# Delta rule: VectorE inverts the first chunk's diagonal blocks, GpSimd begins with the second chunk

## The chip, the cores and the metric

The kernel runs on one core of one Trainium2 chip. The metric is the device time of one execution in microseconds (us); the median of three runs of the kernel before is 3021.94 us (3019.69 to 3023.62). Engines are TensorE (PE), VectorE (DVE), ScalarE (ACT), GpSimd (POOL) and SyncE (SP), which here issues all DMAs. Each engine works through its own queue in order, and they wait for one another on semaphores.

## The reference, cut to what matters

Two layers on a stream of 2 x 1024 tokens of 512 features, each sublayer behind a layernorm and added to the stream: attention by a gated delta rule, a feed-forward with 4-bit weights, latent attention, a sparse feed-forward. The change is in the first. Its core, per batch and head (6 heads of 64):

```
def step(S, inputs):
    q_t, k_t, v_t, g_t, b_t = inputs
    S = S * exp(g_t)
    kv = einsum('bhk,bhkv->bhv', k_t, S)
    u = b_t * (v_t - kv)
    S = S + einsum('bhk,bhv->bhkv', k_t, u)
    o_t = einsum('bhk,bhkv->bhv', q_t * scale, S)
```

over all 1024 steps.

## The kernel before, in words

`four_sublayers` runs the sublayers one after another. In the first, `project_front` computes the projections and writes the convolved q, k and v to a tensor in HBM; `delta_rule` then does the recurrence in 8 chunks of 128 steps (`CHUNKS`), for 12 pairs of batch and head (`BH`) together. Within a chunk the recurrence is a triangular system of 128 unknowns per pair. Its matrix is built from key products (`key_blocks` on VectorE, line 1491, into `a_t`), and query products give `att` (`query_blocks`, line 1500). The four diagonal blocks of 32 x 32 (`BASE`) of each of the 12 matrices are inverted directly; the rest is done on TensorE.

The diagonal blocks travel so. SyncE's `take_blocks(c)` waits until VectorE has written all 12 matrices of the chunk (`a_done`), copies the blocks to HBM (line 912) and back as `base_l`, one block to a partition (line 914): 4 x 12 = 48 partitions, 0 to 47 for even chunks and 64 to 111 for odd ones (`base_rows`). `start_base` has put identity matrices into `base_t`. GpSimd then runs 31 steps of elimination. Step j multiplies column j of `base_l` by row j of `base_t` into `base_tmp` (line 979) and subtracts that from the rows below (line 984), both over (31 - j) x (j + 1) elements of each partition, each instruction waiting for the one before it. At a chunk's end it raises `base_done`. ScalarE transposes the result (`turn_blocks`, line 1312, `tt_done`), and SyncE's `give_blocks(c)` writes both to HBM (line 924) and scatters them into the block-diagonal `diag` and `diag_t` (line 930). TensorE's `off_blocks(c)` (line 1087) waits for `diag`, and `apply_blocks(c)` (line 1118) for `diag_t`.

The order on each engine is written out by hand. The chunks 0 and 1 are prepared in a prologue; turn c of the main loop then solves chunk c and prepares chunk c + 2.

- SyncE: `take_blocks(0)`, load of chunk 2, `take_blocks(1)`, `give_blocks(0)`; then in turn c a load, `take_blocks(c + 2)`, `give_blocks(c + 1)`.
- GpSimd: three memsets, then the inversion of chunks 0 to 7.
- VectorE: for the chunks 0 and 1 the norms, `values_and_keys`, `key_blocks`, `query_blocks`; then `w_lo` (line 1617); then turn 0, which begins with `decay_queries(2)` (line 1434), with `refine_solution(0, ...)` (line 1510) behind it and `norms(2)` (lines 1411 to 1468).
- ScalarE: after its part of the prologue it copies the decayed queries of chunk 1 (line 1304), casts `w_hi` (line 1371), waits for `w_lo_done`, and only then does `turn_blocks(0)`; turn 0 follows with the squares of chunk 2's queries (line 1275) and `copy_off_blocks` (line 1323).
- TensorE: in the prologue, after the query products of chunk 1, `turn_decayed_queries(1)` (line 1073), which waits for eight of VectorE's query blocks; turn 0 begins with `turn_queries(2)`, which waits for all twelve, and `off_blocks(0)`.

Of the kernel before, what the change touches and what calls it, by code (L numbers as in the profile page):

```python
# [23 lines left out]
ALU = mybir.AluOpType  # L24
# [91 lines left out]
def inverse_deviation(pool, norm, rows, group):  # L116

    pool.wait_ge(norm.moments, 7 * group + 7)
    pool.tensor_tensor(norm.rstd[:, rows], norm.var[:, rows], norm.power[:, rows], ALU.pow).then_inc(norm.rstd_done, 1)
# [308 lines left out]
CHUNKS = SEQ // CHUNK  # L428
# [3 lines left out]
BASE = 32  # L432
# [337 lines left out]
def delta_rule(nc, stream, ident, mask, hidden, qkv, beta, decay, eye, w_out, token_norm, fp4, codes, scales):  # L770
# [10 lines left out]
    with Scope(nc, "dr", give_back=True) as s:  # L781
# [3 lines left out]
        NB = QUARTERS * BH  # L785
# [18 lines left out]
        a_t = fp4.weight[:].rearrange("p u (h t) -> p u h t", t=P)  # L804
        base_l, base_t = s.sb("base_l", [P, BASE, BASE]), s.sb("base_t", [P, BASE, BASE])
        base_tt, base_tmp = s.sb("base_tt", [P, BASE, BASE]), s.sb("base_tmp", [P, BASE * BASE // 4])
        diag, diag_t = s.sb("diag", [P, BH, P]), s.sb("diag_t", [P, BH, P])
        m_t = s.sb("m_t", [P, BH, P])
        z = s.sb("z", [P, 2, BH, HEAD_DIM0])
# [15 lines left out]
        l_out, l_in = s.sem("l_out"), s.sem("l_in")  # L825
        t_init = [s.sem(f"t_init{u}") for u in range(2)]
        t_out, tt_out, diag_in, diag_t_in = (s.sem(x) for x in ("t_out", "tt_out", "diag_in", "diag_t_in"))
        w_hi_done, w_lo_done, const_done, zero_done = (s.sem(x) for x in ("w_hi_done", "w_lo_done", "const_done", "zero_done"))
# [5 lines left out]
        d_ps, d_done, kk_ps, qk_ps, a_done, att_done = (s.sem(x) for x in ("d_ps", "d_done", "kk_ps", "qk_ps", "a_done", "att_done"))  # L834
        evens_done = s.sem("evens_done")
        qg_ps, qg_copied = s.sem("qg_ps"), s.sem("qg_copied")
        base_step, base_done, tt_done = s.sem("base_step"), s.sem("base_done"), s.sem("tt_done")
        y_ps, y_done, m_ps, m_done = (s.sem(x) for x in ("y_ps", "y_done", "m_ps", "m_done"))
        z_ps, z_done, w_ps, w_done, x_ps, x_done = (s.sem(x) for x in ("z_ps", "z_done", "w_ps", "w_done", "x_ps", "x_done"))
# [39 lines left out]
        def base_rows(c):  # L879

            return slice(64 * (c % 2), 64 * (c % 2) + NB)
# [9 lines left out]
        STEPS = 2 * (BASE - 1)  # L891
# [72 lines left out]
        @block.gpsimd  # L964
        def _(pool):
            pool.memset(diag[:], 0.0).then_inc(zero_done, 1)
            pool.memset(diag_t[:], 0.0).then_inc(zero_done, 1)
            pool.memset(m_t[:], 0.0).then_inc(zero_done, 1)
            for c in range(CHUNKS):
                rows = base_rows(c)  # L970
                pool.wait_ge(l_in, 16 * (c + 1))
                pool.wait_ge(t_init[c % 2], 16 * (c // 2 + 1))
                for j in range(BASE - 1):
                    left, done = BASE - 1 - j, j + 1
                    shape = [NB, left, done]
                    update = base_tmp[rows, 0:left * done].rearrange("p (r c) -> p r c", r=left)
                    if c or j:
                        pool.wait_ge(base_step, STEPS * c + 2 * j)
                    pool.tensor_tensor(update, base_l[rows, j, j + 1:].unsqueeze(2).broadcast_to(shape),  # L979
                                       base_t[rows, j, 0:done].unsqueeze(1).broadcast_to(shape),  # L980
                                       ALU.mult).then_inc(base_step, 1)
                    pool.wait_ge(base_step, STEPS * c + 2 * j + 1)
                    target = base_t[rows, j + 1:, 0:done]
                    pool.tensor_tensor(target, target, update, ALU.subtract).then_inc(base_step, 1)
                pool.wait_ge(base_step, STEPS * (c + 1))
                pool.sem_inc(base_done, 1)
            pool.memset(token_norm.power[:], -0.5).then_inc(token_norm.power_done, 1)
            pool.wait_ge(token_norm.power_done, 1)
            inverse_deviation(pool, token_norm, EARLY, 0)
# [414 lines left out]
        def _(dve):  # L1404
# [22 lines left out]
            def decay_queries(c):  # L1427
                if c:
                    dve.wait_ge(qg_ps, 2 * c)
                else:  # L1430
                    dve.wait_ge(e_all_done, 1)
                for b in range(BATCH):
                    dve.wait_ge(q_squared, 2 * c + b + 1)
                    dve.tensor_tensor(heads(q_gt[:, b, :]), bank_of_heads(2 + b), along(e_of(0, b, c)),
                                      ALU.mult).then_inc(qg_done, 1)

            def sum_queries(c):
                dve.wait_ge(q_squared, 2 * c + 2)
                dve.tensor_reduce(sums[:, 0, :], square[:, 0].rearrange("p b (h d) -> p (b h) d", d=HEAD_DIM0),
                                  AX.X, ALU.add).then_inc(summed, 1)  # L1440

            def decay_keys(c, b):
                dve.wait_ge(k_squared, 2 * c + b + 1)
                dve.tensor_tensor(rhs[:, c % 3, 1, own(b), :], bank_of_heads((4, 2)[b]), along(e_of(0, b, c)),
                                  ALU.mult).then_inc(bk_done, 1)

            def sum_keys(c):
                dve.wait_ge(k_squared, 2 * c + 2)
                dve.tensor_reduce(sums[:, 1, :], square[:, 1].rearrange("p b (h d) -> p (b h) d", d=HEAD_DIM0),
                                  AX.X, ALU.add).then_inc(summed, 1)  # L1450
                dve.wait_ge(summed, 3 * c + 2)
                dve.tensor_scalar(sums[:], sums[:], 1e-6, None, ALU.add).then_inc(summed, 1)
                dve.wait_ge(summed, 3 * c + 3)
                dve.reciprocal(weight[:], sums[:, 1, :]).then_inc(small, 1)
                dve.wait_ge(small, 6 * c + 1)
                dve.tensor_tensor(by_batch(weight), by_batch(weight), of_chunk(beta[:], c), ALU.mult).then_inc(small, 1)
                dve.wait_ge(small, 6 * c + 2)
                dve.tensor_tensor(by_batch(k_weight), by_batch(weight),
                                  of_chunk(e_all[:, 1, :].rearrange("p (i h) -> p i h", h=HEADS0), c),
                                  ALU.mult).then_inc(small, 1)  # L1460
# [21 lines left out]
            def key_blocks(c):  # L1482
                dve.wait_ge(d_done, FOURS * c + 3)
                if c >= 2:
                    dve.wait_ge(m_ps, FOURS * (c - 1))
                    dve.wait_ge(l_out, 16 * QUARTERS * (c - 1))
                for g, group in enumerate(GROUPS):
                    dve.wait_ge(kk_ps, FOURS * c + g + 1)
                    for i in group:
                        place = PLACE[i][1] * P  # L1490
                        dve.scalar_tensor_tensor(out=a_t[:, c % 2, i, :], in0=banks[KK_BANKS[g]][:, place:place + P],
                                                 scalar=weight[:, i:i + 1], in1=att[:, c % 3, i, :],
                                                 op0=ALU.mult, op1=ALU.mult).then_inc(a_done, 1)

            def query_blocks(c):
                for g, group in enumerate(GROUPS):
                    dve.wait_ge(qk_ps, FOURS * c + g + 1)
                    for i in group:
                        place = PLACE[i][1] * P
                        dve.scalar_tensor_tensor(out=att[:, c % 3, i, :], in0=banks[QK_BANKS[g]][:, place:place + P],  # L1500
                                                 scalar=weight[:, i:i + 1], in1=att[:, c % 3, i, :],
                                                 op0=ALU.mult, op1=ALU.mult).then_inc(att_done, 1)
# [86 lines left out]
            def first_codes(nibble, ops):  # L1589
# [12 lines left out]
                if 2 in ops:  # L1602
                    dve.wait_ge(fp4.step, at + 2)
                    fp4.scaled(dve, nibble).then_inc(fp4.step, 1)

            for c in range(2):
                decay_queries(c)
                sum_queries(c)
                for b in range(BATCH):
                    decay_keys(c, b)  # L1610
                sum_keys(c)
                norms(c)
                values_and_keys(c)
                key_blocks(c)
                query_blocks(c)
            dve.wait_ge(w_hi_done, 1)
            dve.tensor_tensor(w_lo[:], w32, w_hi[:].bitcast(F32), ALU.subtract).then_inc(w_lo_done, 1)
# [1284 lines left out]
```

## Time and profile before

| | |
|---|---|
| median of three runs | 3021.94 us |
| the profiled execution | 3021.52 us |
| its span (first to last instruction) | 3019.7 us |
| busy in it: PE, DVE, ACT, POOL | 94%, 56%, 36%, 26% |
| delta rule, main loop | about 240 to 560 us |
| chunk 0's inversion on GpSimd | ends at about 239.6 us |

Times in the rows are microseconds from the start of the span. A row of the view in order of time gives start, duration from the first of its instructions to the last, engine, line, operation, output and inputs, how often, and in square brackets how long the engine sat idle before it and what ended that. SPq is SyncE's queue issuing DMAs. Releasers are inferred from semaphore events.

### The profile page before, as it was taken

To read this page: it belongs to the slowest core of one execution; us is meant where nothing else is said; L and a number is where in the kernel's file an instruction comes from. 1 tells how busy PE (TensorE), PEld (TensorE's weight loads), DVE (VectorE), ACT (ScalarE), POOL (GpSimd) and SP (SyncE) were. 2 spreads that over 40 slices of the span, in tenths; PEclk is the share of its full clock that TensorE was granted. 3 is DMA by queue.
4 is the path that set the end of the run, shared out by engine and by line. 5 is a ranking of instruction groups with operands and counts; after the bars stand their busy time and mean duration, and the time that the engine had idled before them with its cause. 6 is when DMAs were issued, how large, how long until landed. Compare 5 with 4: busy or idle time off the path is not lost. (4 is left out here: it accounts for less than half of the span.)

```text
span 3019.7 us, 37185 instructions
## 1 busy us (share of the span) xinstructions
PE 2829.2 (94%) x13750; PEld 2332.9 (77%) x13750; DVE 1702.2 (56%) x2585; ACT 1073.9 (36%) x1615; POOL 791.4 (26%) x832
## 2 busy tenths in 40 slices
PE   7966988799999999999999689999999899999998
PEld 7846777678888888888888558888888677888887
DVE  6864677564445444454543666666666256545554
ACT  3343343131121211111211357777777522212221
POOL 0038686100000000000000157777778510000000
PEclk9967999899999999999999889999999999999999
DMA  2243232110000100000100121111110100101001
GB/s 85 104 115 70 52 73 49 46 42 21 22 21 21 42 21 21 21 21 21 35 7 1 40 64 43 43 43 36 43 36 22 43 14 28 42 1 42 14 14 42
DMA packets 96418, 114.92 MB, mean 38 GB/s; under 512 B 47072, under 2 KB 73696, under 8 KB 94624
## 3 DMA queue, kind: packets, MB, share of 16 engines
q1 hardware_dynamic: 96288, 113.20, 12.7%
q8 instruction: 80, 1.31, 0.2%
q14 instruction: 50, 0.41, 0.0%
HBM read 86.16 MB, written 26.74 MB: 37 GB/s over the span
## 5 line engine op out<-in xcount | busy, mean ns | idle before, releaser
L2017 POOL TENSOR_TENSOR att_p_lo<-att_probs,att_p_hi 128x768 fp32r<-128x768 f32 x256 | 467.3, 1837 | 147.3 <-ACT att_p_hi L2074 146.1
L2170 DVE TENSOR_REDUCE att_top<-att_q_scores 128x1 f32<-128x1024 f32 x250 | 305.5, 1222 | 220.0 <-PE att_q_scores L2277 187.9
L271 DVE TENSOR_TENSOR fp_hidden<-fp_gelu,fp_up 128x512 f32<-128x512 f32 x128 | 88.0, 687 | 440.2 <-PE fp_up L75 377.2
L2085 ACT ACTIVATE att_probs<-att_k_scores 128x1024 f32<-128x1024 f32 x256 | 262.9, 1027 | 160.9 <-PE att_k_scores L2295 159.5
L1751 POOL MEMSET lat_power<- 128x16 f32 x1 | 0.1, 111 | 1051.8 <-POOLq L52 1051.8
L256 DVE TENSOR_TENSOR k_stream<-k_stream,fp_down 128x512 f32<-128x512 f32 x256 | 175.4, 686 | 89.6 <-PE fp_down L75 86.1
L335 ACT ACTIVATE fp_gelu<-fp_gate 128x512 f32<-128x512 f32 x128 | 76.4, 597 | 420.3 <-PE fp_gate L75 419.4
L2074 ACT CAST att_p_hi<-att_probs 128x768 fp32r<-128x768 f32 x256 | 211.7, 827 | 0.0
L73 PE MATMUL fp_gate<-fp_feat_hi,fp_w_hi 128*128 128x512 f32 x512 | 200.6, 392 | 4.0 <-DVE fp_feat_lo L241 4.0
L2277 PE MATMUL att_q_scores<-att_k_stack,att_q_stack 128*128 128x512 f32 x500 | 187.1, 456 | 14.5 <-DMA att_q_stack<-att_k_stack 10.6
L75 PE MATMUL fp_gate<-fp_feat_hi,fp_w_lo 128*128 128x512 f32 x512 | 200.2, 391 | 0.0
L74 PE MATMUL fp_gate<-fp_feat_lo,fp_w_hi 128*128 128x512 f32 x512 | 200.1, 391 | 0.0
L73 PE MATMUL fp_up<-fp_feat_hi,fp_w_hi 128*128 128x512 f32 x512 | 199.4, 389 | 0.0
L74 PE MATMUL fp_up<-fp_feat_lo,fp_w_hi 128*128 128x512 f32 x512 | 199.4, 389 | 0.0
L73 PE MATMUL fp_down<-fp_w_hi,fp_h_hi 128*128 128x512 f32 x512 | 199.3, 389 | 0.0
L75 PE MATMUL fp_up<-fp_feat_hi,fp_w_lo 128*128 128x512 f32 x512 | 199.2, 389 | 0.0
L75 PE MATMUL fp_down<-fp_w_hi,fp_h_lo 128*128 128x512 f32 x512 | 199.2, 389 | 0.0
L74 PE MATMUL fp_down<-fp_w_lo,fp_h_hi 128*128 128x512 f32 x512 | 199.2, 389 | 0.0
L2616 DVE TENSOR_TENSOR la_values<-sp_silu,sp_up 128x512 f32<-128x512 f32 x64 | 43.9, 687 | 226.2 <-PE sp_up L75 225.3
L2295 PE MATMUL att_k_scores<-att_q_stack,att_k_stack 128*128 128x512 f32 x512 | 165.0, 403 | 1.7 <-DVE att_top L2170 1.3
L2314 PE MATMUL att_out_rest<-att_probs,att_whole_values 128*128 128x256 f32 x512 | 152.0, 378 | 0.0
L979 POOL TENSOR_TENSOR dr_base_tmp<-dr_base_l,dr_base_t 48x31 f32<-48x31 f32 (+15 forms) x248 | 124.9, 504 | 89.2 <-DMA dr_base_l<-blocks_l 70.1
(350 smaller groups left out, 6537.3 us busy)
## 6 DMA issues: line engine op xcount, KB each, us to landing
f_early<-codes SPq DMA_DIRECT2D x16, 768.0 KB
f_early<-scales SPq DMA_DIRECT2D x16, 768.0 KB
la_values<-w_sparse SPq DMA_DIRECT2D x10, 1024.0 KB, 5.2
f_early<-qkv SPq DMA_DIRECT2D x16, 576.0 KB, 6.2
att_q_stack<-rotated SPq DMA_DIRECT2D x128, 64.0 KB, 2.6
att_k_stack<-rotated SPq DMA_DIRECT2D x128, 64.0 KB, 2.6
qkv<-f_early SPq DMA_DIRECT2D x12, 512.0 KB, 2.9
k_stream<-hidden SPq DMA_DIRECT2D x4, 1024.0 KB, 10.3
```

The costliest lines, as they stand in the source:

```text
L73: pe.matmul(out, w_hi, x_hi, start=start, stop=False)
L74: pe.matmul(out, w_hi, x_lo, start=False, stop=False)
L75: return pe.matmul(out, w_lo, x_hi, start=False, stop=stop)
L256: dve.tensor_tensor(tile, tile, down_ps[j][:], ALU.add).then_inc(added, 1)
L979: pool.tensor_tensor(update, base_l[rows, j, j + 1:].unsqueeze(2).broadcast_to(shape), base_t[rows, j, 0:done].unsqueeze(1).broadcast_to(s ...
L2017: pool.tensor_tensor(p_lo[:, buffer, :], probs[:, slot, 0:SPLIT], p_hi[:, buffer, :].bitcast(F32), ALU.subtract).then_inc(lo_done, 1)
L2074: act.copy(p_hi[:, buffer, :], probs[:, slot, 0:SPLIT]).then_inc(hi_done, 1)
L2085: act.activation(probs[:, t, :], k_scores[:], ACT.Exp).then_inc(exp_done, 1)
L2170: dve.tensor_reduce(top[buffer][:, STACK + t:STACK + t + 1], scores[:], AX.XY, ALU.max, negate=True).then_inc(max_done, 1)
L2277: last = pe.matmul(scores[:, half, :], q_stack[j][:, t * P:(t + 1) * P], k_stack[j][:, half * TB:(half + 1) * TB], start=True, stop=True)
L2295: last = pe.matmul(k_scores[:, half, :], k_stack[j][:, t * P:(t + 1) * P], q_stack[j][:, half * TB:(half + 1) * TB], start=True, stop=True)
L2314: pe.matmul(out_rest[:, 1, 0:REST], whole_values[:, buffer, t, :], probs[:, t, SPLIT:], start=t == 0, stop=t == T - 1).then_inc(out_done, 1)
```

## The change

VectorE gets a function `first_base` with the same 31 steps for chunk 0, on the same tensors and partitions, and calls it in its prologue between `key_blocks(1)` and `query_blocks(1)`. GpSimd's loop over chunks starts at 1; before it stands a wait for its own memsets, and before chunk 1's increment of `base_done` a wait for chunk 0's. The semaphore `first_step` orders the new instructions.

```diff
             pool.memset(m_t[:], 0.0).then_inc(zero_done, 1)
-            for c in range(CHUNKS):
+            pool.wait_ge(zero_done, 3)
+            for c in range(1, CHUNKS):
...
-                    if c or j:
-                        pool.wait_ge(base_step, STEPS * c + 2 * j)
+                    if c > 1 or j:
+                        pool.wait_ge(base_step, STEPS * (c - 1) + 2 * j)
...
-                pool.wait_ge(base_step, STEPS * (c + 1))
+                pool.wait_ge(base_step, STEPS * c)
+                if c == 1:
+                    pool.wait_ge(base_done, 1)
                 pool.sem_inc(base_done, 1)
...
+            def first_base():
+                rows = base_rows(0)
+                dve.wait_ge(l_in, 16)
+                dve.wait_ge(t_init[0], 16)
+                for j in range(BASE - 1):
+                    left, done = BASE - 1 - j, j + 1
+                    shape = [NB, left, done]
+                    update = first_tmp[rows, 0:left * done].rearrange("p (r c) -> p r c", r=left)
+                    if j:
+                        dve.wait_ge(first_step, 2 * j)
+                    dve.tensor_tensor(update, base_l[rows, j, j + 1:].unsqueeze(2).broadcast_to(shape),
+                                      base_t[rows, j, 0:done].unsqueeze(1).broadcast_to(shape),
+                                      ALU.mult).then_inc(first_step, 1)
+                    dve.wait_ge(first_step, 2 * j + 1)
+                    target = base_t[rows, j + 1:, 0:done]
+                    dve.tensor_tensor(target, target, update, ALU.subtract).then_inc(first_step, 1)
+                dve.wait_ge(first_step, STEPS)
+                dve.sem_inc(base_done, 1)
...
                 key_blocks(c)
+                if c:
+                    first_base()
                 query_blocks(c)
```

`first_tmp` is the same tensor as `base_tmp`; the two engines use different partitions of it for these two chunks.

## Rows read from the trace of the kernel before

**Rows 1.** the waits of TensorE, 200 to 262 us: total, times, longest, in us

```profile
PE dr_bank L1087 <- DMA dr_diag<-blocks_t: 24.0, 1, 24.0
```

**Rows 2.** SyncE's queue in order of time, from 180 us

```profile
218.51 0.31 SPq L914 DMA_DIRECT2D dr_base_l<-blocks_l  x1
239.68 0.31 SPq L924 DMA_DIRECT2D blocks_t<-dr_base_t  x1
242.18 1.85 SPq L930 DMA_DIRECT2D dr_diag<-blocks_t  x4
...
276.94 0.36 SPq L924 DMA_DIRECT2D blocks_t<-dr_base_t  x1
```

**Rows 3.** TensorE in order of time, from 190 us

```profile
218.81 1.51 PE L1073 MATMUL dr_bank<-k_ident,dr_q_gt 128*128 128x128 f32 x6 [0.22 <-DVE dr_att L1500]
...
245.86 5.07 PE L1087 MATMUL dr_bank<-f_weight,dr_diag 128*128 128x128 f32 x24 [24.00 <-DMA dr_diag<-blocks_t]
...
286.80 2.84 PE L1087 MATMUL dr_bank<-f_weight,dr_diag 128*128 128x128 f32 x24
```

**Rows 4.** ScalarE in order of time, from 190 us

```profile
220.74 1.48 ACT L1371 CAST dr_w_hi<-dr_att 128x1536 fp32r<-128x1536 f32 x1
239.70 1.93 ACT L1312 COPY dr_base_tt<-dr_base_t 48x1024 f32<-48x1024 f32 x1 [17.48 <-POOLq L986]
241.53 0.85 ACT L1275 ACTIVATE dr_square<-dr_bank 128x384 f32<-128x384 f32 x2
...
250.97 1.14 ACT L1323 COPY dr_m_t<-dr_bank 32x384 f32<-32x384 f32 x3 [0.15 <-PE dr_bank L1087]
```

**Rows 5.** GpSimd in order of time, from 195 us

```profile
222.31 2.17 POOL L979 TENSOR_TENSOR dr_base_tmp<-dr_base_l,dr_base_t 48x252 f32<-48x252 f32 x1
...
254.49 0.61 POOL L979 TENSOR_TENSOR dr_base_tmp<-dr_base_l,dr_base_t 48x252 f32<-48x252 f32 x1
...
279.56 0.23 POOL L979 TENSOR_TENSOR dr_base_tmp<-dr_base_l,dr_base_t 48x31 f32<-48x31 f32 x1 [3.17 <-DMA dr_base_l<-blocks_l]
```

**Rows 6.** DMA issues of 180 to 560 us: count, KB each, median us to landing

```profile
dr_base_l<-blocks_l SPq DMA_DIRECT2D x8, 192.0 KB, 2.9
```

**Rows 7.** VectorE in order of time, prologue of chunk 1

```profile
212.12 3.19 DVE L1491 SCALAR_TENSOR_TENSOR f_weight<-dr_bank,dr_weight,dr_att 128x128 f32<-128x128 f32 x12 [2.24 <-PE dr_bank L1048]
216.51 3.25 DVE L1500 SCALAR_TENSOR_TENSOR dr_att<-dr_bank,dr_weight,dr_att 128x128 f32<-128x128 f32 x12 [1.20 <-PE dr_bank L1048]
222.25 1.76 DVE L1617 TENSOR_TENSOR dr_w_lo<-dr_att,dr_w_hi 128x1536 fp32r<-128x1536 f32 x1 [2.49 <-ACT dr_w_hi L1371]
```

**Rows 8.** VectorE in order of time, two dependent small instructions of chunk 0

```profile
186.42 0.18 DVE L1413 SCALAR_TENSOR_TENSOR dr_correction<-dr_correction,dr_sums 128x24 f32<-128x24 f32 x1
186.63 0.18 DVE L1415 SCALAR_TENSOR_TENSOR dr_norm<-dr_correction,dr_norm 128x24 f32<-128x24 f32 x1
```

**Rows 9.** line 1568, 285 to 480 us, then 540 to 560: ns min/median/max

```profile
L1568 DVE TENSOR_TENSOR dr_o_n<-dr_o_n,dr_o_norm x10: 870/941/1018, 293.5 to 478.1; 128x384 f32<-128x384 f32 x10
...
L1568 DVE TENSOR_TENSOR dr_o_n<-dr_o_n,dr_o_norm x2: 552/555/558, 556.9 to 557.3; 128x384 f32<-128x384 f32 x2
```

**Rows 10.** GpSimd and VectorE in order of time, near 293 us

```profile
293.30 0.65 POOL L979 TENSOR_TENSOR dr_base_tmp<-dr_base_l,dr_base_t 48x247 f32<-48x247 f32 x1
293.49 1.81 DVE L1568 TENSOR_TENSOR dr_o_n<-dr_o_n,dr_o_norm 128x384 f32<-128x384 f32 x2
```

**Rows 11.** GpSimd by line, 239.7 to 267.45 us: count | busy us, mean ns | idle

```profile
L984 POOL TENSOR_TENSOR dr_base_t<-dr_base_t,dr_base_tmp 48x220 f32<-48x220 f32 (+15 forms) x22 | 12.7, 578 | 1.7
L979 POOL TENSOR_TENSOR dr_base_tmp<-dr_base_l,dr_base_t 48x220 f32<-48x220 f32 (+15 forms) x22 | 11.5, 523 | 1.9 <-POOL dr_base_t L984 0.3
```

**Rows 12.** VectorE in order of time, `norms(2)` in turn 0

```profile
262.74 0.54 DVE L1415 SCALAR_TENSOR_TENSOR dr_norm<-dr_correction,dr_norm 128x24 f32<-128x24 f32 x1
...
263.40 0.57 DVE L1466 TENSOR_SCALAR dr_q_norm<-dr_norm 128x12 f32<-128x12 f32 x1
```

**Rows 13.** the waits of TensorE, 540 to 560 us

```profile
PE dr_bank L1087 <- DMA dr_diag<-blocks_t: 8.2, 1, 8.2
```

More of the change, by code:

```diff
@@ L806, in delta_rule @@
         base_tt, base_tmp = s.sb("base_tt", [P, BASE, BASE]), s.sb("base_tmp", [P, BASE * BASE // 4])
+        first_tmp = base_tmp
         diag, diag_t = s.sb("diag", [P, BH, P]), s.sb("diag_t", [P, BH, P])
@@ L836, in delta_rule @@
         qg_ps, qg_copied = s.sem("qg_ps"), s.sem("qg_copied")
+        first_step = s.sem("first_step")
         base_step, base_done, tt_done = s.sem("base_step"), s.sem("base_done"), s.sem("tt_done")
@@ L981, in _ @@
                                        ALU.mult).then_inc(base_step, 1)
-                    pool.wait_ge(base_step, STEPS * c + 2 * j + 1)
+                    pool.wait_ge(base_step, STEPS * (c - 1) + 2 * j + 1)
                     target = base_t[rows, j + 1:, 0:done]
                     pool.tensor_tensor(target, target, update, ALU.subtract).then_inc(base_step, 1)
-                pool.wait_ge(base_step, STEPS * (c + 1))
+                pool.wait_ge(base_step, STEPS * c)
+                if c == 1:
+                    pool.wait_ge(base_done, 1)
                 pool.sem_inc(base_done, 1)
```

## The prediction

> **What bounds the kernel now.** The edit touches one place, the start of the delta rule, so the views to read are the waits of that stretch, then the queues and engines in order of time. The waits [rows 1] show the largest stall of the stage: TensorE's first `off_blocks` matmul stands 24.0 us until `diag` has landed. GpSimd ends chunk 0 at about 239.6, 0.1 before SyncE writes `base_t` out at 239.68, issues four scatters from 242.18 [rows 2], and TensorE starts `off_blocks(0)` at 245.86 [rows 3]. ScalarE's `turn_blocks(0)` stands 17.5 us for the same inversion and starts at 239.70; then come two squares and the copies of the off blocks, of which the last three end at 250.97 + 1.14 = 252.1 [rows 4]. So the bound in chunk 0 is the inversion's end.
>
> GpSimd begins chunk 1 at once, ends it at 276.4, and then waits 3.17 us, to 279.56, for chunk 2's blocks [rows 5]. From there it never hands a backlog on. SyncE writes chunk 1 out at 276.94 [rows 2], behind `take_blocks(2)` in its queue; TensorE reaches `off_blocks(1)` at 286.80 without a wait [rows 3]. Chunk 1's inversion is hidden, if barely (0.5 us), and being early with it buys nothing: `give_blocks(1)` cannot pass `take_blocks(2)`, which waits for VectorE's third set of key blocks.
>
> **What is removed.** 62 GpSimd instructions for chunk 0, done at 239.6. GpSimd's chunk 1 may start when its blocks land instead of behind chunk 0: `base_l` is asked for at 218.51 [rows 2], and such a transfer takes 2.9 [rows 6], so at about 221.4. The added wait on `zero_done` costs nothing (three memsets at the start of the scope, done while GpSimd waits for its first blocks), nor does the one on `base_done` ahead of chunk 1's increment, if VectorE is done by then.
>
> **What is added: 62 chained VectorE instructions.** They start when `key_blocks(1)` ends, 212.12 + 3.19 = 215.3 [rows 7]; chunk 0's blocks are long there (at 222 GpSimd was past the middle of them [rows 5]). Elements per partition: step j has (j+1)(31-j), twice; over 31 steps 2 x 5456 = 10912. The trace of before has no such instruction on VectorE, so I take the nearest. Two dependent small ones of 24 elements start 0.21 us apart, each lasting 0.18 [rows 8]; 384 elements from SBUF twice last 0.555 when alone [rows 9]. 0.555 less 0.18 over 360 elements is 1.04 ns an element, that is 0.96 a ns. So one chained instruction costs 0.188 + n/960 us, and the loop alone 62 x 0.188 + 10912/960 = 11.7 + 11.4 = 23.0 us, ending at 238.4. That is only 1.2 us ahead of GpSimd's 239.6.
>
> **What the two engines do to each other** is the term that decides. The same line, L1568, lasts 552 to 558 ns in the last turn, where GpSimd has finished, and 870 to 1018 ns in all ten cases in which GpSimd was inverting [rows 9]. It reads two tensors from SBUF, as every instruction of the new loop does. One such case is [rows 10]: GpSimd's 293.30 instruction ends at 293.95, and VectorE's pair, issued at 293.49, takes 1.81, where twice 0.555 is 1.11. The other way, `w_lo` at 222.25 for 1.76 us stretches a GpSimd instruction of 252 elements that began 0.06 behind it from 0.61 to 2.17, ending 0.47 after `w_lo` [rows 5, 7]. So they take turns: a blocked GpSimd instruction needs its duration less 0.14 after VectorE's end, a blocked VectorE instruction n/960 and about 0.015 after GpSimd's. In a turn of one each, the new loop pays n/960 + (d - 0.125) for a GpSimd duration d, or n/960 + 0.188 if that is more.
>
> The sum: until 221.1 VectorE is alone and does 18 instructions (18 x 0.188 + 2310/960 = 5.8). 44 are left, with 8602/960 = 9.0 us of data. They alternate with GpSimd's first 44 of chunk 1, which are 12.7 + 11.5 = 24.2 us [rows 11]; less 0.125 each, with the short first ones held at 0.188, 18.9 us. Ending: 221.1 + 9.0 + 18.9 = 249.0, that is 9.4 us after GpSimd's end of before. Bounds: no interference, 238.4; each VectorE instruction waits out a whole GpSimd one, 221.1 + 9.0 + 24.2 = 254.3. Beyond these, the loop's reads are broadcasts and its writes short rows, of which no VectorE row speaks; at twice the time an element it is 11.4 more. I take 249.0, by the rows of L1568 and `w_lo`.
>
> The Trainium skill bears on this (SBUF — State Buffer, section "Who interferes with whom"): a VectorE instruction with two SBUF inputs contends with a GpSimd one that reads SBUF, and whoever is first holds the shared port for the whole instruction. The rows of L1568 agree in kind; taken literally for the whole instruction it gives the upper end, 254.3, where `w_lo`'s case leaves 0.14 of overlap. It speaks against putting the two halves of this work side by side.
>
> **What is queued behind the loop.** `query_blocks(1)` and `w_lo`: before they started at 216.51 and 222.25 [rows 7], before chunk 0's inversion was done, and cost nothing. Now they follow it. `query_blocks(1)` starts at 249.1, 32.6 later; its inputs wait already. The path runs on over TensorE's transposes (218.81 before [rows 3]), ScalarE's two copies and `w_hi` cast (220.74 [rows 4]) to `w_lo` at 222.25 + 32.6 = 254.9, say 0.3 lost to GpSimd, done 256.9. `turn_blocks(0)` waits for exactly that: 257.0 to 258.9, then two squares (0.85) and nine copies in a row (3 x 1.14), last one done at 263.2 against 252.1. Meanwhile `diag` lands 6.3 after the inversion, 255.3; TensorE's first four products need 2 us more, so 257.4, before ScalarE is free at 259.8. ScalarE's chain, not the DMA, is late last, and the shift is 11.1 us.
>
> **What is given back.** GpSimd's chunk 1 now ends near 260 instead of 276.4. VectorE's small chained instructions of turn 0, on which TensorE waits, lost time to it: 0.54 and 0.57 where such ones take 0.18 [rows 8, 12], 0.8 us together. That is gone. The rest of the turns moves as a whole, since GpSimd's later chunks wait for blocks from VectorE. The last turn, where TensorE stands 8.2 us for `diag` [rows 13], moves with chunk 7's blocks.
>
> Net +10.3 us. The profiled execution took 3021.5 (span 3019.7), so 3031.8 by it, and by the median of 3021.9 it is 3032.2; I say 3032.
>
> **Rivals.**
> - The engines do not hinder each other here (48 rows each, in different partitions). Then the loop ends at 238.4, `turn_blocks(0)` starts at 246.1, the copies end at 252.3: +0.2, 3022. For it: the rows of L1568 and `w_lo` are of 128 partitions. Against: GpSimd had 48 rows in them and still blocked all 128. Chance 0.14.
> - Faster: the waits on itself cost VectorE nothing. Two independent ones of a line follow each other at about n/960 + 0.06 (the twelve `key_blocks` of 128 elements in 3.19 us [rows 7] are 0.27 each, 0.13 of it fixed, so 0.06 is generous); the loop would end at 215.4 + 62 x 0.06 + 11.4 = 230.5, and the copies near 244.4, 7.7 earlier: 3014. It decides below about 0.18 us fixed per instruction, with no lock at all. Against: the 0.21 pitch in [rows 8]. Chance 0.03.
> - Worse: whole-instruction turns (254.3, so +15.6, 3037) or slow short rows (up to +22, 3044 and more). Chance 0.18.
> - Forecast: 0.65, its own range 3028 to 3036 (the end of the loop 246 to 253).
>
> A measurement of this kernel tells no change from one of 0.2%, 6 us. The forecast and the worse case lie over 3028; a little of the forecast's low side falls under it. Slower 0.80, same 0.16, faster 0.04. TensorE's clock in turn 0 may move one or two us either way, as its idle times move. Range for 8 in 10: 3025 to 3038.
>
> **What would show it.** In the changed profile: VectorE's new lines from 215.3 with 0.2 + n/960 until about 221, then the larger ones at 0.6 to 0.8 each; end at 249; GpSimd's chunk 1 from 221.5, its durations longer by about VectorE's n/960 less 0.2; `w_lo` near 255, `turn_blocks(0)` near 257, `off_blocks(0)` near 255, `off_blocks(1)` near 297 without a wait. It is wrong if the new instructions keep 0.16 + n/960 with GpSimd running (first rival), if they start later than 215.3, or if later turns change their length.

## The result and the profile after

The changed kernel takes 3029.97 us (median of 20 runs, 3022.4 to 3040.7), the kernel before 3021.99 (median of 20, 3014.3 to 3028.0): a ratio of 1.0027, interval 1.0018 to 1.0036, so 5 to 11 us slower. 3032 was forecast, with a range of 3025 to 3038. The profiled execution took 3032.7, 11.2 more than that of before.

The busy times on the page of the kernel after:

```profile
PE 2833.0 (93%) x13750; PEld 2336.8 (77%) x13750; DVE 1732.7 (57%) x2647; ACT 1074.0 (35%) x1615; POOL 760.1 (25%) x770
```

GpSimd has 62 instructions fewer than before and VectorE 62 more. VectorE in order of time, from the new loop on (line 1621 multiplies, line 1626 subtracts; line 1505 is `query_blocks`, line 1643 `w_lo`):

```profile
214.57 0.17 DVE L1621 TENSOR_TENSOR dr_base_tmp<-dr_base_l,dr_base_t 48x31 f32<-48x31 f32 x1
...
222.43 0.42 DVE L1626 TENSOR_TENSOR dr_base_t<-dr_base_t,dr_base_tmp 48x240 f32<-48x240 f32 x1
...
226.82 0.60 DVE L1626 TENSOR_TENSOR dr_base_t<-dr_base_t,dr_base_tmp 48x256 f32<-48x256 f32 x1
...
232.37 0.67 DVE L1626 TENSOR_TENSOR dr_base_t<-dr_base_t,dr_base_tmp 48x240 f32<-48x240 f32 x1
...
247.51 0.63 DVE L1621 TENSOR_TENSOR dr_base_tmp<-dr_base_l,dr_base_t 48x31 f32<-48x31 f32 x1
248.18 0.18 DVE L1626 TENSOR_TENSOR dr_base_t<-dr_base_t,dr_base_tmp 48x31 f32<-48x31 f32 x1
248.52 3.19 DVE L1505 SCALAR_TENSOR_TENSOR dr_att<-dr_bank,dr_weight,dr_att 128x128 f32<-128x128 f32 x12 [0.16 <-DVE dr_base_t L1626]
254.26 1.76 DVE L1643 TENSOR_TENSOR dr_w_lo<-dr_att,dr_w_hi 128x1536 fp32r<-128x1536 f32 x1 [2.55 <-ACT dr_w_hi L1376]
...
272.93 0.18 DVE L1420 SCALAR_TENSOR_TENSOR dr_norm<-dr_correction,dr_norm 128x24 f32<-128x24 f32 x1
...
273.24 0.17 DVE L1471 TENSOR_SCALAR dr_q_norm<-dr_norm 128x12 f32<-128x12 f32 x1
```

The loop lasts from 214.57 to 248.36, 33.8 us. The same size, 240 elements, takes 0.42 us at 222.43 and 0.67 at 232.37, and 31 elements, 0.17 at the start, take 0.63 at 247.51. Beside it, GpSimd (its chunk 1, then the first of chunk 2):

```profile
220.63 0.24 POOL L982 TENSOR_TENSOR dr_base_tmp<-dr_base_l,dr_base_t 48x31 f32<-48x31 f32 x1 [45.12 <-DMA dr_base_l<-blocks_l]
...
254.32 1.96 POOL L982 TENSOR_TENSOR dr_base_tmp<-dr_base_l,dr_base_t 48x135 f32<-48x135 f32 x1
...
259.72 0.25 POOL L987 TENSOR_TENSOR dr_base_t<-dr_base_t,dr_base_tmp 48x31 f32<-48x31 f32 x1
289.11 0.23 POOL L982 TENSOR_TENSOR dr_base_tmp<-dr_base_l,dr_base_t 48x31 f32<-48x31 f32 x1 [29.14 <-DMA dr_base_l<-blocks_l]
```

GpSimd ends chunk 1 at 259.97 instead of 276.4 and then stands 29.14 us for chunk 2's blocks, where it stood 3.17 [rows 5]: the head start went into waiting. The instruction of 254.32 lasts 1.96 us, because `w_lo` holds it, as `w_lo` held one instruction of chunk 0 before. What follows the loop, first SyncE's queue, then TensorE (line 1078 `turn_decayed_queries(1)`, 1092 `off_blocks`), then ScalarE (1317 `turn_blocks`, 1280 the squares, 1328 the copies):

```profile
248.49 0.31 SPq L926 DMA_DIRECT2D blocks_t<-dr_base_t  x1
250.98 1.85 SPq L932 DMA_DIRECT2D dr_diag<-blocks_t  x4
```

```profile
250.82 1.51 PE L1078 MATMUL dr_bank<-k_ident,dr_q_gt 128*128 128x128 f32 x6 [32.88 <-DVE dr_att L1505]
...
255.69 5.49 PE L1092 MATMUL dr_bank<-f_weight,dr_diag 128*128 128x128 f32 x24 [1.82 <-DMA dr_diag<-blocks_t]
...
296.13 2.84 PE L1092 MATMUL dr_bank<-f_weight,dr_diag 128*128 128x128 f32 x24
```

```profile
256.05 1.95 ACT L1317 COPY dr_base_tt<-dr_base_t 48x1024 f32<-48x1024 f32 x1 [1.82 <-DVE dr_w_lo L1643]
257.90 0.85 ACT L1280 ACTIVATE dr_square<-dr_bank 128x384 f32<-128x384 f32 x2
258.66 2.28 ACT L1328 COPY dr_m_t<-dr_bank 32x384 f32<-32x384 f32 x6
261.22 1.14 ACT L1328 COPY dr_m_t<-dr_bank 32x384 f32<-32x384 f32 x3 [0.28 <-PE dr_bank L1092]
```

`off_blocks(0)` starts at 255.69 instead of 245.86 [rows 3], the last copy ends at 262.36 instead of 252.1 [rows 4], and `off_blocks(1)` starts at 296.13 instead of 286.80, again without a wait: +9.8, +10.2, +9.3.

These shifts count from the start of the span, and 0.83 us of them arises ahead of the changed code: `key_blocks(0)` starts at 192.37 instead of 191.54. From there to `key_blocks(1)` the kernel after is 1.5 us quicker, 19.1 instead of 20.6. VectorE, before and then after:

```profile
191.54 3.19 DVE L1491 SCALAR_TENSOR_TENSOR f_weight<-dr_bank,dr_weight,dr_att 128x128 f32<-128x128 f32 x12 [2.25 <-PE dr_bank L1048]
...
206.73 0.37 DVE L1415 SCALAR_TENSOR_TENSOR dr_norm<-dr_correction,dr_norm 128x24 f32<-128x24 f32 x1
```

```profile
192.37 3.19 DVE L1496 SCALAR_TENSOR_TENSOR f_weight<-dr_bank,dr_weight,dr_att 128x128 f32<-128x128 f32 x12 [2.25 <-PE dr_bank L1053]
...
207.13 0.18 DVE L1420 SCALAR_TENSOR_TENSOR dr_norm<-dr_correction,dr_norm 128x24 f32<-128x24 f32 x1
...
211.46 3.19 DVE L1496 SCALAR_TENSOR_TENSOR f_weight<-dr_bank,dr_weight,dr_att 128x128 f32<-128x128 f32 x12 [1.67 <-PE dr_bank L1053]
```

GpSimd does nothing here any more, so the small instructions of `norms(1)` lose no time to it: together they save 0.9 us. The other 0.6 is on TensorE, whose 24 key products take 3.62 us instead of 4.20 (mean granted clock 0.58 instead of 0.50). Counted from `key_blocks(0)`, `off_blocks(1)` is late by 8.5.

### The profile page after: what moved, and what is told of

The parts are those of the page before. It is cut to its first block and busy times, and to the rows that moved or that the text cites. A ratio compares the mean times of both kernels' runs of the same rounds, so it can differ in the third digit from the quotient of the medians.

```text
span 3030.9 us, 37185 instructions
## 1 busy us (share of the span) xinstructions
PE 2833.0 (93%) x13750; PEld 2336.8 (77%) x13750; DVE 1732.7 (57%) x2647; ACT 1074.0 (35%) x1615; POOL 760.1 (25%) x770
## 5 line engine op out<-in xcount | busy, mean ns | idle before, releaser
L2303 PE MATMUL att_q_scores<-att_k_stack,att_q_stack 128*128 128x512 f32 x500 | 187.5, 457 | 13.7 <-DMA att_q_stack<-att_k_stack 10.3
L321 ACT CAST fp_w_hi<-f_weight 128x1536 fp32r<-128x1536 f32 x32 | 47.1, 1476 | 279.6 <-DVE f_weight L150 279.6
## 6 DMA issues: line engine op xcount, KB each, us to landing
k_stream<-hidden SPq DMA_DIRECT2D x4, 1024.0 KB, 10.3
```

What stands on the lines that cost most here:

```text
L2303: last = pe.matmul(scores[:, half, :], q_stack[j][:, t * P:(t + 1) * P], k_stack[j][:, half * TB:(half + 1) * TB], start=True, stop=True)
```

## The experiments

Each is told by its ratio to runs of the kernel before on the same chip, where it was timed, and by the places in its trace, which say more: a turn's length moves by some us with the clock (see the end). Line numbers in the rows are each kernel's own; the instructions are those above.

**hold: GpSimd waits for VectorE's last step.**

```diff
             pool.wait_ge(zero_done, 3)
+            pool.wait_ge(base_done, 1)
             for c in range(1, CHUNKS):
```

> The changed kernel, but GpSimd waits for VectorE's last step of chunk 0 before it starts chunk 1; nothing else differs. Theory P (the two engines take turns at a shared SBUF port): VectorE's loop starts at 214.6 and takes 62 x 0.188 + 10912/960 = 23.0 us instead of 33.8, so ends near 237.6; turn_blocks(0) near 245.4, off_blocks(1) near 286.5, total within 2 us of the kernel before (3022). GpSimd's chunk 1 ends near 276, where SyncE gets to it. Rival Q (the loop's short rows and broadcasts are slow on VectorE by themselves, or GpSimd's early start matters): the loop stays near 33.8 us, and the total 8 us over the kernel before or more.

Measured: 3019.1 us, ratio 0.9993 (0.9982 to 1.0004). VectorE, then GpSimd:

```profile
213.78 0.17 DVE L1622 TENSOR_TENSOR dr_base_tmp<-dr_base_l,dr_base_t 48x31 f32<-48x31 f32 x1
...
221.65 0.40 DVE L1627 TENSOR_TENSOR dr_base_t<-dr_base_t,dr_base_tmp 48x240 f32<-48x240 f32 x1
...
236.41 0.18 DVE L1627 TENSOR_TENSOR dr_base_t<-dr_base_t,dr_base_tmp 48x31 f32<-48x31 f32 x1
```

```profile
236.79 0.24 POOL L983 TENSOR_TENSOR dr_base_tmp<-dr_base_l,dr_base_t 48x31 f32<-48x31 f32 x1 [62.65 <-DVEq L1629]
```

The loop takes 22.8 us, with 0.40 for 240 elements. So its access patterns cost nothing extra. The inversion ends at 236.59, 3.0 us earlier than before, but `off_blocks(0)` starts at 244.24, only 1.6 earlier, because the last scatter into `diag` landed later (at most 3.6 us after its issue, before 2.3; see the end). The total is that of the kernel before, so the whole loss of the change is made by GpSimd running beside the loop. Q falls; GpSimd's early start by itself loses nothing either, for all_psum keeps it.

**all_psum: side by side, but no instruction with two SBUF inputs.**

```diff
+                for u, bank in enumerate((1, 7)):
+                    dve.tensor_copy(banks[bank][rows, :].rearrange("p (r c) -> p r c", r=half),
+                                    base_l[rows, u * half:(u + 1) * half, :]).then_inc(first_copied, 1)
+                dve.wait_ge(first_copied, 2)
                 for j in range(BASE - 1):
...
+                    column = banks[(1, 7)[j // half]][rows, BASE * (j % half) + j + 1:BASE * (j % half + 1)]
-                    update = first_tmp[rows, 0:left * done].rearrange("p (r c) -> p r c", r=left)
+                    update = banks[6][rows, 0:left * done].rearrange("p (r c) -> p r c", r=left)
...
-                    dve.tensor_tensor(update, base_l[rows, j, j + 1:].unsqueeze(2).broadcast_to(shape),
+                    dve.tensor_tensor(update, column.unsqueeze(2).broadcast_to(shape),
```

> The changed kernel, with GpSimd inverting chunk 1 alongside as there, but VectorE first copies the blocks of base_l into two PSUM banks (two instructions of 512 elements, 1.4 us in all) and keeps the product in a third, so that no instruction of its loop reads two tensors from SBUF. Theory P: no turns are taken; the loop's instructions last 0.16 to 0.2 + n/960 with GpSimd running, and end near 239.3; GpSimd's chunk 1 takes its 36.5 us undisturbed, from 220.6 to about 257; total 1 to 2 us over the kernel before. Rival Q2 (any work of the two engines side by side slows both, by semaphores or memory in general): the loop stays near 34 us plus the copies, total +9.

Measured: 3019.4 us, ratio 0.9990 (0.9980 to 1.0001). VectorE and GpSimd of the same time:

```profile
230.35 0.41 DVE L1627 TENSOR_TENSOR dr_bank<-dr_bank,dr_base_t 48x240 f32<-48x240 f32 x1
230.80 0.40 DVE L1632 TENSOR_TENSOR dr_base_t<-dr_base_t,dr_bank 48x240 f32<-48x240 f32 x1
...
238.46 0.18 DVE L1632 TENSOR_TENSOR dr_base_t<-dr_base_t,dr_bank 48x31 f32<-48x31 f32 x1
```

```profile
220.53 0.24 POOL L982 TENSOR_TENSOR dr_base_tmp<-dr_base_l,dr_base_t 48x31 f32<-48x31 f32 x1 [45.18 <-DMA dr_base_l<-blocks_l]
...
258.25 0.25 POOL L987 TENSOR_TENSOR dr_base_t<-dr_base_t,dr_base_tmp 48x31 f32<-48x31 f32 x1
```

With GpSimd inverting chunk 1 from 220.5, 240 elements take 0.41 and 0.40 in the two lines, and the loop 22.9 us after the copies. GpSimd takes 38.0, of which 1.6 is `w_lo`'s, so 36.4, where the kernel before took 36.6. Side by side costs neither engine anything here, as VectorE reads one SBUF tensor at a time. Q2 falls.

**tmp_psum: only the product in PSUM** (the middle edit of all_psum alone).

> The changed kernel with only the product (base_tmp of chunk 0) in a PSUM bank: the multiplications still read two tensors from SBUF, the subtractions one. Theory P: within one loop, with GpSimd running, the multiplications are stretched (240 elements: 0.4 to 0.7 us) and the subtractions are not (240 elements: 0.41 to 0.45). The loop ends between 241 and 246. Rival Q2: both are stretched alike, as in the changed kernel.

Measured: 3023.3 us in a single run, inside the spread of the kernel before; the loop takes 24.8 us and ends at 238.83, earlier than the 241 to 246 expected. VectorE, then one GpSimd instruction:

```profile
227.75 0.83 DVE L1621 TENSOR_TENSOR dr_bank<-dr_base_l,dr_base_t 48x252 f32<-48x252 f32 x1
228.62 0.41 DVE L1626 TENSOR_TENSOR dr_base_t<-dr_base_t,dr_bank 48x252 f32<-48x252 f32 x1
229.06 0.42 DVE L1621 TENSOR_TENSOR dr_bank<-dr_base_l,dr_base_t 48x247 f32<-48x247 f32 x1
...
238.22 0.39 DVE L1621 TENSOR_TENSOR dr_bank<-dr_base_l,dr_base_t 48x31 f32<-48x31 f32 x1
```

```profile
229.07 0.86 POOL L987 TENSOR_TENSOR dr_base_t<-dr_base_t,dr_base_tmp 48x207 f32<-48x207 f32 x1
```

Within one loop the line that reads two SBUF tensors (1621) is stretched to 0.83 for 252 elements, and the line that reads one (1626) takes 0.41 at the same size. That half held. It is the reads that count and not the write: the stretched line writes to PSUM, the other to SBUF. The size did not hold. From 229 to about 236 each multiplication began just ahead of a GpSimd instruction or near its end and ran nearly free (247 elements: 0.42 at 229.06), and now GpSimd paid: its instruction of 229.07 took 0.86 for 207 elements, which take 0.58 to 0.60 in the kernel before. Less `w_lo`'s 1.4, GpSimd's chunk takes 38.2 instead of 36.4. So the cost fell on the engine that came second.

**handover: GpSimd begins chunk 0, VectorE ends it.** This is the version to which the above points: the pieces one behind the other, each where its engine would idle.

```diff
+        FIRST = 15
...
-            for c in range(1, CHUNKS):
+            for c in range(CHUNKS):
                 rows = base_rows(c)
+                if c == 1:
+                    pool.wait_ge(base_done, 1)
...
-                for j in range(BASE - 1):
+                for j in range(FIRST if c == 0 else BASE - 1):
...
-                dve.wait_ge(l_in, 16)
-                dve.wait_ge(t_init[0], 16)
-                for j in range(BASE - 1):
+                dve.wait_ge(base_step, 2 * FIRST)
+                for j in range(FIRST, BASE - 1):
...
                 key_blocks(c)
+                query_blocks(c)
                 if c:
                     first_base()
-                query_blocks(c)
```

(GpSimd's waits on `base_step` are counted anew, and for chunk 0 only VectorE raises `base_done`), and `w_lo`, with ScalarE's wait for it, moved into turn 0:

```diff
-            act.wait_ge(w_lo_done, 1)
             turn_blocks(0)
...
                 if ahead:
+                    if c == 0:
+                        act.wait_ge(w_lo_done, 1)
                     exponent_of_decays(ahead)
...
-            dve.wait_ge(w_hi_done, 1)
-            dve.tensor_tensor(w_lo[:], w32, w_hi[:].bitcast(F32), ALU.subtract).then_inc(w_lo_done, 1)
...
                 if ahead:
                     sum_queries(ahead)
+                if c == 0:
+                    dve.wait_ge(w_hi_done, 1)
+                    dve.tensor_tensor(w_lo[:], w32, w_hi[:].bitcast(F32), ALU.subtract).then_inc(w_lo_done, 1)
```

> Another split of the same work: GpSimd does steps 0 to 14 of chunk 0 as before (from 201.5), VectorE takes steps 15 to 30 after query_blocks(1), GpSimd holds chunk 1 until that is done, and w_lo and ScalarE's wait for it are moved behind chunk 0's inversion. Theory P with the path of the prediction: VectorE starts its 32 instructions near 219.5 and needs 32 x 0.188 + 5580/960 = 11.8 us, so base_done near 231.3 instead of 239.6, off_blocks(0) near 237.5, total 7 to 8 us under the kernel before (3014). Rival R (the chain behind the inversion is bound elsewhere, for instance chunk 1's inversion, hidden by 0.5 us only, comes late now): off_blocks(0) is early but off_blocks(1) isn't, and less than 4 us is gained.

Measured: 3012.5 us, ratio 0.9964 (0.9951 to 0.9977): 8.3 us under the kernel before, better than both kernels. VectorE's part, GpSimd's second chunk, `off_blocks(0)`:

```profile
219.87 0.42 DVE L1624 TENSOR_TENSOR dr_base_tmp<-dr_base_l,dr_base_t 48x256 f32<-48x256 f32 x1
...
231.52 0.18 DVE L1629 TENSOR_TENSOR dr_base_t<-dr_base_t,dr_base_tmp 48x31 f32<-48x31 f32 x1
```

```profile
231.84 0.23 POOL L986 TENSOR_TENSOR dr_base_tmp<-dr_base_l,dr_base_t 48x31 f32<-48x31 f32 x1 [12.01 <-DVEq L1631]
```

```profile
238.07 5.49 PE L1095 MATMUL dr_bank<-f_weight,dr_diag 128*128 128x128 f32 x24 [16.20 <-DMA dr_diag<-blocks_t]
```

VectorE's 32 instructions take 11.8 us; `off_blocks(0)` starts 7.8 earlier than before and `off_blocks(1)` (277.05) 9.7 earlier. R falls.

**handover_wlo: the same without moving `w_lo`.**

> The handover kernel with w_lo and ScalarE's wait for it left where they were in the kernel before. VectorE's last step again ends near 231.6, w_lo follows to 233.4, turn_blocks(0) near 233.5, still ahead of the diag scatter. If the handover alone makes the gain, off_blocks(0) starts near 238 and the ratio to before is 0.9965 as with the handover kernel; if the moved w_lo made part of it, the gain is smaller by more than 2 us.

Measured: 3011.5 us, ratio 0.9966 (0.9953 to 0.9978). TensorE:

```profile
237.53 5.49 PE L1095 MATMUL dr_bank<-f_weight,dr_diag 128*128 128x128 f32 x24 [15.88 <-DMA dr_diag<-blocks_t]
...
276.97 2.94 PE L1095 MATMUL dr_bank<-f_weight,dr_diag 128*128 128x128 f32 x24 [0.54 <-DMA dr_diag<-blocks_t]
```

The move of `w_lo` made no part of the gain. `off_blocks(1)` now waits 0.54 for `diag`: the 0.5 us by which chunk 1 was hidden are used up (GpSimd ends it at 269.46, and SyncE writes it out at 269.57).

**handover_early: VectorE takes over at step 12, ahead of `query_blocks(1)`** (`FIRST` becomes 12, and the call stays where the change has it).

> The handover kernel with the change of hands at step 12 and ahead of query_blocks(1): VectorE starts at 215.3, does 38 instructions in 38 x 0.188 + 7220/960 = 14.7 us, so base_done near 230.0 against 231.7. off_blocks(0) near 236.4 if the diag path is last; but query_blocks(1), the transposes behind it and ScalarE's copies now end near 236, so at most 1.7 us more than the handover kernel, total 3011 to 3013.

Measured: 3013.4 us, ratio 0.9976 (0.9965 to 0.9986).

```profile
229.62 0.18 DVE L1629 TENSOR_TENSOR dr_base_t<-dr_base_t,dr_base_tmp 48x31 f32<-48x31 f32 x1
```

```profile
237.62 5.49 PE L1095 MATMUL dr_bank<-f_weight,dr_diag 128*128 128x128 f32 x24 [2.31 <-DMA dr_diag<-blocks_t]
```

The inversion ends 1.9 us earlier than in handover and `off_blocks(0)` only 0.45: it starts 7.8 after the inversion's end instead of 6.4. The total is no better than that of the other two; the three intervals overlap.

**free: the changed kernel with `w_lo` moved** (the last edit of handover on the changed kernel).

> The changed kernel with w_lo moved into turn 0 (behind sum_queries(2)) and ScalarE's wait for it moved ahead of exponent_of_decays(2), so that nothing but query_blocks(1) is queued between the loop and turn_blocks(0). Theory of the prediction (ScalarE's chain is late last, at 11.1 us, the DMA path only 9.4): turn_blocks(0) starts near 254.0 instead of 256.05, the last off-block copy ends 1 to 1.5 us earlier than 262.36. Rival D (the diag path and ScalarE's chain end together in this kernel, since the last scatter landed 3.3 us after its issue): the last copy ends within 0.5 us of 262.4 and nothing is gained.

Measured: 3031.9 us in a single run, inside the spread of the changed kernel. Here VectorE's loop ended at 247.46, 0.9 earlier than in the changed kernel. ScalarE:

```profile
253.23 1.92 ACT L1317 COPY dr_base_tt<-dr_base_t 48x1024 f32<-48x1024 f32 x1
...
260.68 1.14 ACT L1328 COPY dr_m_t<-dr_bank 32x384 f32<-32x384 f32 x3 [0.57 <-PE dr_bank L1092]
```

`turn_blocks(0)` starts 2.8 earlier, and the last copy ends 14.4 us after the loop; in the changed kernel it was 14.0. In absolute terms it ends at 261.82, 0.5 earlier than 262.36, and the loop's earlier end accounts for all of that. TensorE is what ScalarE's copies now wait for. Nothing is gained: the theory's 1 to 1.5 us fails, and D holds.

**before_free: the same edit on the kernel before.**

> The kernel before with w_lo moved the same way. There w_lo held a GpSimd instruction of chunk 0 for 1.56 us. Theory P: chunk 0's inversion ends near 238.1 instead of 239.6, off_blocks(0) starts near 244.3 instead of 245.86, and w_lo, now near 243, holds GpSimd in chunk 1 instead; the total gains 1 to 2 us, less than one look can tell. Rival: w_lo does not hold GpSimd, chunk 0 still ends near 239.6.

Measured: 3027.0 us in a single run, inside the spread of the kernel before. GpSimd, then TensorE:

```profile
237.57 0.24 POOL L984 TENSOR_TENSOR dr_base_t<-dr_base_t,dr_base_tmp 48x31 f32<-48x31 f32 x1
...
242.32 1.85 POOL L979 TENSOR_TENSOR dr_base_tmp<-dr_base_l,dr_base_t 48x156 f32<-48x156 f32 x1
```

```profile
244.34 5.15 PE L1087 MATMUL dr_bank<-f_weight,dr_diag 128*128 128x128 f32 x24 [22.06 <-DMA dr_diag<-blocks_t]
```

Chunk 0 takes 36.3 us instead of 37.8 and `off_blocks(0)` starts 1.5 earlier, while an instruction of chunk 1 now lasts 1.85, with `w_lo` running. The places are as expected; the total can't be told.

## Why the prediction was right

**The term that decides, the turns.** The loop was put at 33.7 us (215.3 to 249.0) and took 33.8; alone it was put at 23.0 and took 22.8 in hold. That it is two SBUF inputs, and not running side by side, is shown by all_psum. The Trainium skill's rule (SBUF — State Buffer, section "Who interferes with whom") holds in kind; read literally, whole durations, it gave a loop of 39.0 us (215.3 to 254.3), and the trace has 33.8.

**Its shape was a little off.** The sum took n/960 + d - 0.125 throughout, and n/960 + 0.188 where that is more. That fits the middle: 0.63 us from start to start for the first of 256 elements, by the formula and in the trace. Over the first 32 of the 44 hindered instructions the trace has 0.4 us less than the formula. Over the next eleven it has 0.9 more, since VectorE's data are so short there that the limit is GpSimd's own pace, one instruction in about 0.7 us, where the formula gives 0.5 to 0.7. The last one ran unhindered, 0.3 less. That these nearly cancel, so that the loop's length came out within 0.1 us, is luck. GpSimd lost only 1.4 us to the loop (39.3 us for chunk 1, less 1.5 of `w_lo`, against 36.4 in all_psum), VectorE 11: each GpSimd instruction began 0.20 us or less before VectorE's ended, and 0.14 of such an overlap costs it nothing by [rows 5, 7]. That is how the two fell into step here, and no rule: in tmp_psum they lost about 2 us each.

**"ScalarE's chain, not the DMA, is late last" was wrong**, though the number was near: +10.2 where 11.1 stood. At the first copies ScalarE was indeed the last, and six follow without a wait at 258.66, but the last three waited 0.28 us for TensorE. `off_blocks(0)` started 7.3 after the inversion's end, where 6.3 was taken from before, and its 24 matmuls took 5.49 us at the low clock (granted 0.50), where before they took 5.07 (mean 0.56, since it rose at about 250). So TensorE's third group and ScalarE ended together, and free shows that taking `w_lo` off ScalarE's path gives nothing.

**What is given back** was put at 0.8. The two instructions of [rows 12] took 0.18 and 0.17, as forecast, and `off_blocks(1)` was late by 9.3 after +10.2 at the last copy: 0.9.

**One gain was overlooked.** The prediction took the loop's start, 215.3, from the trace of before, but the same relief that it counted in turn 0 comes in the prologue too, since GpSimd no longer inverts chunk 0 beside `norms(1)`. From `key_blocks(0)` to `key_blocks(1)` it is 18.9 to 19.3 us in the five kernels in which GpSimd is idle there (after, hold, all_psum, tmp_psum, free) and 20.3 to 20.7 in the five in which it works (before, before_free and the three handovers). So about 1.5 us was missing from the sum. It does not show in the loop's start (214.57, only 0.7 early), as the profiled execution after reached `key_blocks(0)` 0.8 late.

**GpSimd's head start is worth nothing:** right, as the 29.14 us show. **The rest moves as a whole:** right within the noise of the clock. Net +10.3 was forecast, and less the 1.5 overlooked it is +8.8; measured were +8.5 from `key_blocks(0)` to turn 1 and +8.0 by the medians, whose interval of 5 to 11 holds them all.

**The rivals.** No hindrance (0.14) is what all_psum builds, and it comes out at before's time, as that rival priced it (3022); the changed kernel isn't it. The faster rival needed 0.06 us fixed per instruction; hold shows 0.19.

## What to carry to other kernels

Giving half of a chain's work to another engine gains only if the two don't hinder each other: ask of each instruction on VectorE whether it reads two tensors from SBUF while GpSimd reads there too. Here each of those took the time of its data plus nearly one GpSimd instruction, on average 0.25 us more than alone. If they must run together, PSUM as the home of one operand freed both engines here, for 1.3 us of copies. Ask also where the engine that is relieved had been slowing others: those places give time back. Where a critical chain can be cut, it is better to hand it over midway to the faster engine, when that falls idle, than to give each engine a whole one: here that turned +8 us into -8.

## What the runs showed of the hardware that was not expected

The slowest of the four scatters into `diag` took longer to land in the kernels in which TensorE's transposes run at the same time. `diag` DMAs of chunk 0, first before, then after (issue to landing):

```profile
DMA to landing us min/median/max: 1.8/2.2/2.3
```

```profile
DMA to landing us min/median/max: 1.7/2.2/3.3
```

The maximum is 2.3 in handover and handover_wlo and 2.5 in before_free, where TensorE stood over 15 us for it; it is 3.2 to 3.8 in the changed kernel, hold, all_psum, tmp_psum, free and handover_early, where it stood 1.8 to 2.3. In these six VectorE (`query_blocks(1)`, in most also `w_lo`) and ScalarE (its copies) are at work at the same time as well, and no run separates them from the transposes. Why it is so is open.

The length of a turn of the main loop goes with the clock. The same turn 5, before and after (stretch and length; PE, PEld, DVE, ACT, POOL busy; granted clock; DMA):

```profile
470.20:512.00 41.80, 36.64 (x287) 32.33 (x286) 32.99 (x78) 14.33 (x33) 29.42 (x58) 1.00 0.21 47
```

```profile
478.70:525.20 46.50, 41.39 (x288) 36.46 (x287) 32.66 (x79) 14.48 (x33) 30.71 (x60) 0.89 0.19 42
```

At a mean granted clock of 1.00 it takes 41.8 us, at 0.89 46.5, with the same instructions. The other turns from 1 to 5 fit in: 43.6 us at 0.96, 44.6 to 45.4 at 0.92, 46.5 to 47.2 at 0.89. Such dips fall on different turns from run to run. They take the kernel after from 9.3 us late at `off_blocks(1)` to 11.3 late at `off_blocks(7)` (561.90 against 550.65), which is what the two profiled executions are apart, where the medians are 8.0 apart. That is why single runs are read by their places and not by their totals.
